# Attention and expert block on one core: spills of batch 2 sent first, w1 ahead of them, a late norm, and eight dummy matmuls

## The chip, the cores and the metric

One NeuronCore of a Trainium2 chip runs the whole program. Five engines work side by side, each through its own instructions in order: TensorE (PE: matmuls, with PEld for the loading of weights), VectorE (DVE), ScalarE (ACT), GpSimd (POOL) and SyncE (SP), which here only starts DMAs. They wait for each other through semaphores. The metric is device time in microseconds, lower is better.

## The reference

Eight batches of 256 tokens by 128 features go through a cross attention block and then a block of 8 experts. The softmax of the attention runs over the head axis, not over the keys.

```python
def _L0_xattn_ref(Q, K, V, W_Q, W_K, W_V, W_O):
    q, k, v = proj_split(Q, W_Q), proj_split(K, W_K), proj_split(V, W_V)   # 8 heads of 16
    scores = jnp.einsum('bhqd,bhkd->bhqk', q, k) / jnp.sqrt(jnp.float32(dh))
    attn = jax.nn.softmax(scores, axis=1)                                   # over the heads
    ctx = jnp.einsum('bhqk,bhkd->bhqd', attn, v)
    return jnp.einsum('bsd,ed->bse', ctx.transpose(0, 2, 1, 3).reshape(b, s, d), W_O)

def _L0_ffn_ref(x, Wr, br, W1, b1, W2, b2):
    logits = jnp.einsum('btd,de->bte', x, Wr) + br
    gates = jax.nn.softmax(jnp.where(top2_mask, logits, neg_inf), axis=-1)
    h = jax.nn.relu(jnp.einsum('btd,edh->bteh', x, W1) + b1)                # all 8 experts
    return jnp.einsum('bte,bteh,ehd->btd', gates, h, W2) + jnp.einsum('bte,ed->btd', gates, b2)

x = x + _L0_xattn_ref(_layernorm(x), ctx_1024, ctx_1024, ...)
x = x + _L0_ffn_ref(_layernorm(x), ...)
```

## The kernel before

Every engine's order is written out by hand. A function `beginning()` per engine lists the first part of the run step by step, and `period(i)` the steady part; `wait_ge` on semaphores joins the engines. A step is called by its batch and part: batches are counted from 0 (so the second batch is number 1), `u` = 0 to 3 is one of the four key and query quarters of a batch, `e` one of the 8 experts.

For one batch the path is this. TensorE projects keys and queries. ScalarE rounds each into a high part and VectorE makes the low part (`k_lo`, `q_lo`: high and low parts keep the precision). SyncE writes them to DRAM ("spill") and reads them back in another layout as `k_stack` and `q_stack`, which `scores(b, u)` multiplies; batch 0 alone has another path without DRAM. VectorE takes the maximum over the heads (`head_max`), TensorE subtracts it (`subtract_max`), ScalarE takes exponentials. The sum over heads is made on TensorE for batch 0 (`head_sum` on PE, with ident) and on GpSimd after that (three additions: `half_sum`, `quarter_sum`, `e_sum`). ScalarE turns the sum into a reciprocal (`invert_sum`: a logarithm, then an exponential), VectorE multiplies (`normalize`, a 128x1024 product of `e_sb` and `e_rcp`). TensorE applies the values and W_O (`attend_values`, `project_out`), VectorE adds the residual and takes statistics (`add_residual`, `ln2`), GpSimd makes the scale and offset (`ln2_end`), ScalarE the normed rows (`make_x1n`), TensorE transposes them (`transpose_x1n`) and starts the experts: `expert_up(b, e)` is six matmuls in `h_ps`, a ReLU on ScalarE follows, then `expert_down(b, e)` into `y_ps`, and `add_expert(b, e)` on VectorE adds the gated result.

The first layer norm works on all 16 row tiles of x (two per batch) in groups. `ln1(lo, hi, at)` on VectorE makes the statistics and the variance of tiles lo to hi; `ln1_rest` on GpSimd waits for that group's variance and makes scale and offset. The last group, `ln1(5 * TT, NT, 4)`, is tiles 10 to 15, that is batches 5 to 7. `split_w1(e)` makes high and low parts of expert e's first weights, on ScalarE and GpSimd.

`expert_down(b, e)` waits until `add_expert` has freed its half of `y_ps`: `wait(pe, gated, j - 1)` with j = 8b + e. In GpSimd's `beginning()` these steps stand in a row: `head_sum(1, 3)`, `ln1_rest(5 * TT, NT, 4)`, `split_w1(5)`, `head_sum(2, 0)`, `split_w1(6)`, `head_sum(2, 1)`, `ln2_end(1)`. In ScalarE's: `relu(0, 4)`, `invert_sum(2, 0)`, `exponentiate(2, 2)`, `relu(0, 5)`, `invert_sum(2, 1)`, `take_k_hi(4)`, `make_x1n(1)`, `relu(0, 6)`. `keep_warm(n)` on TensorE issues n matmuls of the identity whose result nobody reads.

Of the kernel before, what the change touches and what calls it, by code (L numbers as in the profile page):

```python
# [13 lines left out]
P = 128  # L14
# [3 lines left out]
def build(nc, x, ctx_t, w_attn, wr, br, w1, b1_t, w2, b2, out):  # L18
# [3 lines left out]
    TT = S // P  # L22
    NT = B * TT
# [12 lines left out]
    with ExitStack() as stack:  # L36
# [152 lines left out]
        @block.sync  # L189
        def _(sp):  # L190
            def spill_k(b):
                sp.wait_ge(k_hi_made, b)
                sp.wait_ge(k_lo_made, b)
                for part, spilled in enumerate((k_spilled, k_spilled2)):
                    src = k_parts[:, part, :].bitcast(F32).unsqueeze(1).to_broadcast([P, 2, S])
                    sp.dma_start(k_scratch[b % 2, part], src).then_inc(spilled, 16)

            def spill_q(b):
                sp.wait_ge(q_hi_made, b)
                sp.wait_ge(q_lo_made, b)  # L200
                sp.dma_start(q_scratch[b % 2], q_parts[:].bitcast(F32)).then_inc(q_spilled, 16)

            def load_k_stack(b):
                sp.wait_ge(k_spilled, 16 * b)
                sp.wait_ge(k_spilled2, 16 * b)
                if b > 2:
                    sp.wait_ge(scores_done, UNITS * (b - 1))
                for copy in range(2):
                    src = k_scratch[b % 2, copy].rearrange("(j r) c s -> (r c) j s", r=2 * DH)
                    sp.dma_start(k_stack[64 * copy:64 * copy + 64, b % 2, :, :].bitcast(F32),  # L210
                                 src).then_inc(k_stack_in[b % 2], 16)

            def load_q_stack(b):
                sp.wait_ge(q_spilled, 16 * b)
                if b > 2:
                    sp.wait_ge(scores_done, UNITS * (b - 1))
                if b <= 2:
                    sp.wait_ge(q_zeroed[b % 2], 1)
                src = q_scratch[b % 2].rearrange("(j o d) c s -> o (d c) j s", o=2, d=DH)
                for copy in range(2):  # L220
                    for odd in range(2):
                        row = 64 * copy + 32 * odd
                        sp.dma_start(q_stack[row:row + 32, b % 2, :, odd, :].bitcast(F32),
                                     src[odd]).then_inc(q_stack_in[b % 2], 16)

            def store(b):
                sp.wait_ge(gated, E * (b + 1))
                sp.dma_start(out[b].rearrange("(t p) d -> p t d", p=P), y_out[:, b % 2]).then_inc(stored[b % 2], 16)

            def period(i):  # L230
                if there(i - 5):
                    store(i - 5)
                if i - 1 < B:
                    spill_q(i - 1)
                    load_q_stack(i - 1)
                if i < B:
                    spill_k(i)
                    load_k_stack(i)

            x_rows = x.rearrange("b (t p) d -> p (b t) d", p=P)  # L240
            sp.dma_start(x_all[:, 0:TT, :], x_rows[:, 0:TT, :]).then_inc(x0_in, 16)
            sp.dma_start(ctxT[:, 0, :], ctx_t[0]).then_inc(ctx_in[0], 16)
            spill_k(1)
            sp.dma_start(w1_sb[:], w1.rearrange("e d h -> d e h")).then_inc(w1_in, 16)
            load_k_stack(1)
            spill_q(1)
            load_q_stack(1)
            spill_k(2)
            sp.dma_start(ctxT[:, 3:B, :], ctx_t[3:B].rearrange("b d s -> d b s")).then_inc(ctx_rest_in, 16)
            load_k_stack(2)  # L250
            spill_q(2)
            load_q_stack(2)
            sp.dma_start(w2_sb[:], w2.rearrange("e (c p) d -> p (e c) d", p=P)).then_inc(w2_in, 16)
            spill_k(3)
            load_k_stack(3)
            for i in range(4, PERIODS):
                period(i)
            for k in range(2):
                sp.wait_ge(stored[k], 16 * len(range(k, B, 2)))

        @block.tensor
        def _(pe):
            def keep_warm(n):
                for _ in range(n):
                    nc.tensor.matmul(score_ps[:, 1, 0:P], ident[:], ident[:], start=True, stop=True, skip_group_check=True)  # L265

            def project_k(b, freed, n):
                wait(pe, freed, n)
# [69 lines left out]
            def subtract_max(b, u):  # L338
                if UNITS * b + u == 0:
                    pe.wait_ge(neg_ident_made, 1)  # L340
                pe.wait_ge(max_made, UNITS * b + u + 1)
                m4 = shift_m[:, u % 2, :].unsqueeze(1).to_broadcast([P, BANK // P, P])
                for half in range(2):
                    mm = nc.tensor.matmul(score_ps[:, u % 2, half * BANK:(half + 1) * BANK], neg_ident[:], m4,  # L344
                                          start=False, stop=True, skip_group_check=True)
                mm.then_inc(shifted, 1)
# [136 lines left out]
            def beginning():  # L483
# [26 lines left out]
                project_v(1, v_taken, 1)  # L510
                scores(1, 1)
                subtract_max(1, 0)
                attend_values(0, q_lo_made, 2)
                subtract_max(1, 1)
                project_out(0, heads_taken, 1)
                project_v(2, x1_made, 1)
                scores(1, 2)
                scores(1, 3)
                transpose_x1n(0, v_taken, 3)
                subtract_max(1, 2)  # L520
                expert_up(0, 0)
# [312 lines left out]
        def _(dve):  # L834
# [43 lines left out]
            def q_lo(b):  # L878
                low_part(q_parts[:, 1, :], q_bank(b), q_parts[:, 0, :], q_hi_made, b, q_lo_made)
# [161 lines left out]
            def beginning():  # L1041
                dve.wait_ge(x1_in, 16)
                ln1(TT, 2 * TT, 1)
                spread_q(0)
                ln1_end(1, 1)
                k_lo(1)
                spread_q(1)
                head_max(0, 0)
                head_max(0, 1)
                dve.wait_ge(x_in, 16)  # L1050
                ln1(2 * TT, 3 * TT, 2)
                k_lo(2)
                q_lo(1)
                head_max(0, 2)
                ln1(3 * TT, 5 * TT, 3)
                head_max(0, 3)
                normalize(0, 0)
                normalize(0, 1)
                split_wr()
                q_lo(2)  # L1060
                normalize(0, 2)
                head_max(1, 0)
                normalize(0, 3)
                head_max(1, 1)
                ln1(5 * TT, NT, 4)
                add_residual(0)
                ln2(0)
                head_max(1, 2)
                head_max(1, 3)
                x1T_low(0)  # L1070
                normalize(1, 0)
                head_max(2, 0)
                take_logits(0)
                choose_experts(0)
                normalize(1, 1)
                k_lo(3)
                head_max(2, 1)
                make_gates(0)
                transpose_gates(0)
                normalize(1, 2)  # L1080
                normalize(1, 3)
                q_lo(3)
                add_expert(0, 0)
                head_max(2, 2)
                add_expert(0, 1)
                add_expert(0, 2)
                add_b2(0)
                head_max(2, 3)
                add_residual(1)
                ln2(1)  # L1090
                add_expert(0, 3)
                normalize(2, 0)
                k_lo(4)
                head_max(3, 0)
                x1T_low(1)
                add_expert(0, 4)
                add_expert(0, 5)
                take_logits(1)
                normalize(2, 1)
                choose_experts(1)  # L1100
                add_expert(0, 6)
                head_max(3, 1)
                q_lo(4)
                normalize(2, 2)
                add_expert(0, 7)
                normalize(2, 3)
                make_gates(1)
                transpose_gates(1)
                add_expert(1, 0)
                head_max(3, 2)  # L1110
                add_expert(1, 1)
                add_residual(2)
                ln2(2)
                add_expert(1, 2)
                k_lo(5)
                normalize(3, 0)
                add_b2(1)
                head_max(3, 3)
                add_expert(1, 3)
                normalize(3, 1)  # L1120
                x1T_low(2)
                add_expert(1, 4)
# [143 lines left out]
```

## Time and profile before

| what | value |
|---|---|
| median of 3 runs | 211.2 us (210.09 to 212.29) |
| the profiled execution | 212.29 us, span in the profile 210.4 us |
| mean granted clock of TensorE | 0.992 of full speed |
| TensorE busy | 199.6 us, 95% |
| VectorE, ScalarE, GpSimd busy | 80%, 63%, 54% |
| share of the ending chain on TensorE | 91% |

The span is the time between the first and last instruction of the profiled execution; the 1.9 us between it and 212.29 lie around the program. TensorE is busy nearly throughout, and the chain of work that ended last runs through it almost alone from 40 us on. Times in rows are counted from the start of the span.

### The profile page before, as it was taken

Reading aid. Unit: us, or ns where it says so; the run is one execution under the profiler, and the core shown is the slowest. Engines: PE = TensorE matmul, PEld = TensorE weight load, DVE = VectorE, ACT = ScalarE, POOL = GpSimd, SP = SyncE. Lnnn points to the kernel's source line nnn. Section 1 sums busy time; section 2 is a strip of 40 time slices with the busy share of each in tenths; the row PEclk is TensorE's granted clock in tenths of the full one; section 3 lists DMA queues with packets and bytes.
Section 4 is the critical chain, followed back from the end, with each engine's and each line's share of the span. In section 5 each row is a group of like instructions: output and inputs, shape, how many; then the busy total and the mean of one; then the engine's idle time right before and its main releaser. Section 6 shows DMA issues by size and latency. Waiting matters only on the chain.

```text
span 210.4 us, 4952 instructions
## 1 busy us (share of the span) xinstructions
PE 199.6 (95%) x1736; PEld 176.7 (84%) x1736; DVE 167.7 (80%) x453; ACT 132.3 (63%) x316; POOL 112.8 (54%) x132
## 2 busy tenths in 40 slices
PE   6999977698999999999999999999999999999994
PEld 6845865596799978997999889998998899789993
DVE  6388859878798999899888988898999888556532
ACT  2227738678577856877677767587757776345441
POOL 8502838849976397719662856466746674010000
PEclk9999999979999999999999999999999999999999
DMA  6649586805605163315041503332001000000000
GB/s 182 149 121 273 145 258 183 247 4 163 171 19 166 37 174 99 94 34 154 2 153 51 171 7 121 83 126 50 3 0 28 0 2 0 28 3 2 25 3 25
DMA packets 20248, 18.70 MB, mean 89 GB/s; under 512 B 1760, under 2 KB 18688, under 8 KB 20224
## 3 DMA queue, kind: packets, MB, share of 16 engines
q1 hardware_dynamic: 17472, 16.91, 27.9%
q10 hardware_dynamic: 2752, 1.48, 2.8%
q8 instruction: 14, 0.23, 0.5%
q14 instruction: 10, 0.08, 0.1%
HBM read 11.83 MB, written 6.55 MB: 87 GB/s over the span
## 4 chain that ended last, share of the span: by engine, by line
PE 91%; DVE 3%; issue 2%; ACT 2%; POOL 1%; DVEq 0%; POOLq 0%; ACTq 0%
PE y_ps L417 28%; PE h_ps L404 22%; PE score_ps L344 7%; PE misc_ps L363 6%; PE score_ps L332 6%; PE h_ps L352 3%; PE score_ps L265 3%; PE misc_ps L384 2%; PE score_ps L321 2%; PE score_ps L404 2%; PE misc_ps L372 1%; PE misc_ps L270 1%; PE misc_ps L310 1%; PE misc_ps L289 1%; PE misc_ps L283 1%
## 5 line engine op out<-in xcount | busy, mean ns | idle before, releaser
L671 ACT ACTIVATE hT<-h_ps,b_sb 128x256 f32<-128x256 f32 x118 | 49.4, 470 | 34.1 <-PE h_ps L404 33.0
L417 PE MATMUL y_ps<-w_sb,hT 128*128 128x128 f32 x512 | 68.5, 277 | 0.0
L417 PEld LDWEIGHTS y_ps<-w_sb,hT 128*128 128x128 f32 x512 | 63.3, 191 | 3.4 <-issue 2.2
L1156 POOL TENSOR_TENSOR half_sum<-e_sb 128x512 f32<-128x512 f32 x28 | 37.2, 1328 | 32.0 <-ACT e_sb L643 31.7
L912 DVE TENSOR_TENSOR attn<-e_sb,e_rcp 128x1024 f32<-128x1024 f32 x32 | 42.2, 1321 | 3.3 <-ACT e_rcp L654 3.3
L904 DVE TENSOR_REDUCE shift_m<-score_ps 128x128 fp32r<-128x1024 f32 x32 | 38.7, 1213 | 4.0 <-PE score_ps L332 2.8
L404 PE MATMUL h_ps<-x1T_hi,w_lo 128*128 128x256 f32 x118 | 38.1, 323 | 1.3 <-ACT hT L671 0.6
L643 ACT ACTIVATE e_sb<-score_ps 128x1024 f32<-128x1024 f32 x32 | 32.8, 1024 | 5.6 <-PE score_ps L344 5.4
L978 DVE SCALAR_TENSOR_TENSOR acc<-y_ps,gates,acc 128x128 f32<-128x128 f32 x96 | 29.1, 343 | 8.6 <-PE y_ps L417 7.3
L404 PE MATMUL h_ps<-x1T_hi,w_hi 128*128 128x256 f32 x118 | 33.3, 283 | 0.0
L404 PE MATMUL h_ps<-x1T_lo,w_hi 128*128 128x256 f32 x118 | 33.3, 282 | 0.0
L1158 POOL TENSOR_TENSOR quarter_sum<-half_sum 128x256 f32<-128x256 f32 x28 | 27.5, 983 | 2.2
L404 PEld LDWEIGHTS h_ps<-x1T_hi,w_lo 128*128 128x128 f32 x118 | 22.6, 192 | 4.2 <-issue 2.0
L404 PEld LDWEIGHTS h_ps<-x1T_lo,w_hi 128*128 128x128 f32 x118 | 22.6, 192 | 0.3
L404 PEld LDWEIGHTS h_ps<-x1T_hi,w_hi 128*128 128x128 f32 x118 | 22.6, 191 | 0.0
L332 PE MATMUL score_ps<-q_stack,k_stack 128*128 128x256 f32 x112 | 20.0, 303 | 1.9 <-issue 1.9
L344 PE MATMUL score_ps<-shift_m,neg_ident 128*128 128x512 f32 x64 | 21.8, 421 | 0.0
L1161 POOL TENSOR_TENSOR e_sum<-quarter_sum 128x128 f32<-128x128 f32 x28 | 17.6, 629 | 2.2
L332 PEld LDWEIGHTS score_ps<-q_stack,k_stack 128*128 128x128 f32 x112 | 15.4, 194 | 2.4 <-issue 2.3
L1167 POOL TENSOR_TENSOR ln_rstd<-ln_var,neg_half 128x2 f32<-128x2 f32 x8 | 5.7, 707 | 21.0 <-DVE ln_var L871 21.0
L363 PE MATMUL misc_ps<-attn,v_pad 128*32 128x256 f32 x256 | 15.5, 382 | 0.6 <-issue 0.6
L344 PEld LDWEIGHTS score_ps<-shift_m,neg_ident 128*128 128x128 f32 x64 | 10.1, 193 | 3.1 <-issue 2.8
(112 smaller groups left out, 286.3 us busy)
## 6 DMA issues: line engine op xcount, KB each, us to landing
k_scratch<-k_parts SPq DMA_DIRECT2D x14, 256.0 KB, 2.6
k_stack<-k_scratch SPq DMA_DIRECT2D x14, 256.0 KB, 3.9
q_stack<-q_scratch SPq DMA_DIRECT2D x28, 128.0 KB, 2.7
q_scratch<-q_parts SPq DMA_DIRECT2D x7, 256.0 KB, 2.1
w_sb<-in_w SPq DMA_DIRECT2D x1, 1024.0 KB, 7.1
out_y<-y_out SPq DMA_DIRECT2D x8, 128.0 KB, 1.9
x_all<-in_x ACTq DMA_DIRECT2D x1, 768.0 KB, 6.1
ctxT<-in_ctx_t SPq DMA_DIRECT2D x1, 640.0 KB, 5.1
```

The costliest lines, as they stand in the source:

```text
L332: mm = nc.tensor.matmul(score_ps[:, u % 2, 2 * j * P:(2 * j + 2) * P], k_stack[:, b % 2, j, kt * P:(kt + 1) * P], q_stack[:, b % 2, j, :, ...
L344: mm = nc.tensor.matmul(score_ps[:, u % 2, half * BANK:(half + 1) * BANK], neg_ident[:], m4, start=False, stop=True, skip_group_check=True)
L363: mm = nc.tensor.matmul(misc_ps[32 * g:32 * g + 32, 0:S], v_pad[:, b % 4, kt, h, :], attn[:, b % 2, kt, h, :], start=(odd == 0 and kt == 0 ...
L404: mm = nc.tensor.matmul(hidden(j)[:, c * S:(c + 1) * S], w[:, e, c * P:(c + 1) * P], xt[:, b % 2, :], start=(k == 0), stop=(k == 2))
L417: mm = nc.tensor.matmul(y_ps[:, j % 2, t * D:(t + 1) * D], hT[:, j % 2, c, t * P:(t + 1) * P], w2_sb[:, e * HC + c, :], start=(c == 0), st ...
L643: nc.scalar.activation(e_sb[:, u, :], score_ps[:, u % 2, :], ACT.Exp, scale=SCALE).then_inc(exp_made, 1)
L671: op = nc.scalar.activation(hT[:, j % 2, c, :], hidden(j)[:, c * S:(c + 1) * S], ACT.Relu, bias=b1_sb[:, e * HC + c:e * HC + c + 1])
L904: nc.vector.tensor_reduce(shift_m[:, u % 2, :], score_ps[:, u % 2, :].rearrange("p (h q) -> p q h", h=H), AX.X, ALU.max).then_inc(max_made, 1)
L912: nc.vector.tensor_tensor(attn[:, b % 2, kt, :, qt * P:(qt + 1) * P], e_sb[:, u, :].rearrange("p (h q) -> p h q", h=H), e_rcp[:, u, :].uns ...
L978: op = nc.vector.scalar_tensor_tensor(out=dst, in0=y_ps[:, j % 2, t * D:(t + 1) * D], scalar=gates[:, b % 2, t, e:e + 1], in1=src[:, t, :] ...
L1156: nc.gpsimd.tensor_tensor(half_sum[:], e[:, 0:HQ // 2], e[:, HQ // 2:HQ], ALU.add).then_inc(sum_step, 1)
L1158: nc.gpsimd.tensor_tensor(quarter_sum[:], half_sum[:, 0:HQ // 4], half_sum[:, HQ // 4:HQ // 2], ALU.add).then_inc(sum_step, 1)
```

## The change

Three edits. On SyncE the load of w1 goes ahead of the first spill and gets two waits of its own (`x1_in` and `ctx_in[1]`, two input loads that ScalarE starts), and the spill of the queries of batch 1 goes ahead of its key stack load. On VectorE the statistics of tiles 10 to 15 move from before `add_residual(0)` to behind `q_lo(3)`. On TensorE a new function `fill` issues 2, 2 and 4 dummy matmuls in three places; its wait is for `q_lo_made` of batch 1.

```diff
             sp.dma_start(ctxT[:, 0, :], ctx_t[0]).then_inc(ctx_in[0], 16)
+            sp.wait_ge(x1_in, 16)
+            sp.wait_ge(ctx_in[1], 16)
+            sp.dma_start(w1_sb[:], w1.rearrange("e d h -> d e h")).then_inc(w1_in, 16)
             spill_k(1)
-            sp.dma_start(w1_sb[:], w1.rearrange("e d h -> d e h")).then_inc(w1_in, 16)
+            spill_q(1)
             load_k_stack(1)
-            spill_q(1)
             load_q_stack(1)
...
+            def fill(times):
+                pe.wait_ge(q_lo_made, 1)
+                for _ in range(times):
+                    nc.tensor.matmul(y_ps[:, 0, 0:P], ident[:], ident[:], start=True, stop=True, skip_group_check=True)
...
                 subtract_max(1, 0)
+                fill(2)
                 attend_values(0, q_lo_made, 2)
                 subtract_max(1, 1)
                 project_out(0, heads_taken, 1)
+                fill(2)
                 project_v(2, x1_made, 1)
                 scores(1, 2)
                 scores(1, 3)
+                fill(4)
                 transpose_x1n(0, v_taken, 3)
...
                 head_max(1, 1)
-                ln1(5 * TT, NT, 4)
                 add_residual(0)
...
                 q_lo(3)
+                ln1(5 * TT, NT, 4)
                 add_expert(0, 0)
```

SyncE's queue at its start, before: `k_scratch` and `q_scratch` are the spills of batch 1, `w_sb` is w1, `k_stack` and `q_stack` the loads that `scores(1, 0)` waits for.

```order
3 L196 DMA k_scratch<-k_parts 256x1x256 [waits k_lo_made,k_hi_made]
4 L196 DMA k_scratch<-k_parts 256x1x256
5 L244 DMA w_sb<-in_w 128x8x256
6 L210 DMA k_stack<-k_scratch 64x4x256 [waits k_spilled2,k_spilled]
7 L210 DMA k_stack<-k_scratch 64x4x256
8 L201 DMA q_scratch<-q_parts 128x512 [waits q_lo_made,q_hi_made]
9 L223 DMA q_stack<-q_scratch 32x4x256 [waits q_zeroed1,q_spilled]
```

The same place of the changed kernel:

```order
3 L245 DMA w_sb<-in_w 128x8x256 [waits ctx1_in,x1_in]
4 L196 DMA k_scratch<-k_parts 256x1x256 [waits k_lo_made,k_hi_made]
5 L196 DMA k_scratch<-k_parts 256x1x256
6 L201 DMA q_scratch<-q_parts 128x512 [waits q_lo_made,q_hi_made]
7 L210 DMA k_stack<-k_scratch 64x4x256 [waits k_spilled2,k_spilled]
8 L210 DMA k_stack<-k_scratch 64x4x256
9 L223 DMA q_stack<-q_scratch 32x4x256 [waits q_zeroed1,q_spilled]
```

w1 now stands first, and the query spill stands before the two key stack loads.

VectorE around `add_residual(0)` (L857) before; L912 is `normalize(0, 3)`, L904 `head_max(1, 1)`, and L837 to L844 the statistics of tiles 10 to 15:

```order
40 L912 TENSOR_TENSOR attn<-e_sb,e_rcp 128x8x128 [waits rcp_made]
41 L904 TENSOR_REDUCE shift_m<-score_ps 128x128 [waits scores_done]
42 L837 BN_STATS ln_stats<-x_all 128x6 x6
43 L841 BN_AGGR ln_mv<-ln_stats 128x2 [waits ln1_step]
44 L841 BN_AGGR ln_mv<-ln_stats 128x2 x5
45 L844 TENSOR_SCALAR ln_var<-ln_mv 128x6 [waits ln1_step]
46 L857 TENSOR_TENSOR x<-misc_ps,x_all 128x256 [waits wo_done]
```

VectorE between the products of batch 1 and the first expert's result, in the changed kernel (L922 is `normalize(1, 2)` and `(1, 3)`, L886 `q_lo(3)`, L988 `add_expert(0, 0)`):

```order
69 L922 TENSOR_TENSOR attn<-e_sb,e_rcp 128x8x128 [waits rcp_made] x2
70 L886 TENSOR_TENSOR q_parts<-misc_ps,q_parts 128x256 [waits q_hi_made]
71 L847 BN_STATS ln_stats<-x_all 128x6 x6
72 L851 BN_AGGR ln_mv<-ln_stats 128x2 [waits ln1_step]
73 L851 BN_AGGR ln_mv<-ln_stats 128x2 x5
74 L854 TENSOR_SCALAR ln_var<-ln_mv 128x6 [waits ln1_step]
75 L988 SCALAR_TENSOR_TENSOR acc<-y_ps,gates,x 128x128 [waits gates_made,y_done]
```

The four rows of the statistics now follow `q_lo(3)` and precede the first use of an expert's result; nothing stands between `head_max(1, 1)` and `add_residual(0)` any more.

GpSimd from `head_sum(1, 3)` to `ln2_end(1)` in the changed kernel (L1149 to L1158 is `ln1_rest(5 * TT, NT, 4)`, L1184 `split_w1(5)` and `(6)`, L1177 `ln2_end(1)`):

```order
38 L1171 TENSOR_TENSOR e_sum<-quarter_sum 128x128 [waits sum_step]
39 L1149 TENSOR_TENSOR ln_rstd<-ln_var,neg_half 128x6 [waits ln1_var_made]
40 L1154 TENSOR_TENSOR ln_neg<-ln_mv,minus_one 128x6
41 L1158 TENSOR_TENSOR ln_off<-ln_neg,ln_rstd 128x6 [waits ln1_rstd_made,ln1_off_step]
42 L1184 TENSOR_TENSOR w_lo<-w_sb,w_hi 128x256 [waits w1_hi_made]
43 L1166 TENSOR_TENSOR half_sum<-e_sb 128x512 [waits exp_made]
44 L1168 TENSOR_TENSOR quarter_sum<-half_sum 128x256 [waits sum_step]
45 L1171 TENSOR_TENSOR e_sum<-quarter_sum 128x128 [waits sum_step]
46 L1184 TENSOR_TENSOR w_lo<-w_sb,w_hi 128x256 [waits w1_hi_made]
47 L1166 TENSOR_TENSOR half_sum<-e_sb 128x512 [waits exp_made]
```

Nothing moved here: the order is that of before, with `ln1_rest` in the same place in the row.

## Rows read from the trace of the kernel before

**Rows 1.** The page: the granted clock of TensorE in 40 slices, in tenths.

```profile
PEclk9999999979999999999999999999999999999999
```

**Rows 2.** Timeline of TensorE: start us, us, line, tile; in brackets idle before.

```profile
7.90 1.28 PE L265 MATMUL score_ps<-ident 128*128 128x128 f32 x10
...
27.80 0.72 PE L332 MATMUL score_ps<-q_stack,k_stack 128*128 128x256 f32 x4 [1.90 <-issue]
...
32.31 1.93 PE L363 MATMUL misc_ps<-attn,v_pad 128*32 128x256 f32 x32 [0.61 <-issue]
...
34.83 0.68 PE L372 MATMUL misc_ps<-w_qkvo,headsT 128*128 128x128 f32 x4
36.03 0.71 PE L310 MATMUL misc_ps<-w_qkvo,ctxT 128*128 128x128 f32 x4 [0.52 <-DVE x L857]
...
39.10 0.41 PE L283 MATMUL misc_ps<-ident,x1n 128*128 128x128 f32 x2 [1.41 <-ACT x1n L597]
```

**Rows 3.** By window: PE, PEld, DVE, ACT, POOL busy; then granted clock, DMA share, GB/s.

```profile
41.00:42.00 1.00, 1.00 (x8) 1.00 (x7) 0.70 (x1) 0.55 (x3) 0.87 (x1) 0.64 0.80 219
42.00:43.00 1.00, 1.00 (x7) 1.00 (x7) 0.66 (x1) 0.97 (x4) 0.92 (x2) 0.50 0.01 4
...
44.00:45.00 1.00, 1.00 (x6) 0.86 (x5) 0.93 (x9) 0.53 (x2) 0.19 (x1) 0.65 0.00 0
```

**Rows 4.** Timeline of SyncE's DMA issues; then its waits (total us, times, longest).

```profile
15.89 1.29 SPq L210 DMA_DIRECT2D k_stack<-k_scratch  x2
17.43 0.40 SPq L201 DMA_DIRECT2D q_scratch<-q_parts  x1
23.44 1.76 SPq L223 DMA_DIRECT2D q_stack<-q_scratch  x4
...
SPq L223 <- DMA q_scratch<-q_parts: 16.9, 7, 5.5
...
q_stack<-q_scratch SPq DMA_DIRECT2D x28, 128.0 KB, 2.7
```

**Rows 5.** Timeline of VectorE around both places of the moved statistics.

```profile
33.26 1.25 DVE L837 BATCH_NORM_STATS2 ln_stats<-x_all 128x6 f32<-128x128 f32 x6
...
35.55 0.42 DVE L857 TENSOR_TENSOR x<-misc_ps,x_all 128x256 f32<-128x256 f32 x1
...
52.57 0.42 DVE L876 TENSOR_TENSOR q_parts<-misc_ps,q_parts 128x256 fp32r<-128x256 f32 x1
52.91 0.60 DVE L978 SCALAR_TENSOR_TENSOR acc<-y_ps,gates,x 128x128 f32<-128x128 f32 x2
```

**Rows 6.** Timeline of GpSimd: late scale and offset, splits, sums, and `ln2_end(0)`.

```profile
37.07 0.71 POOL L1167 TENSOR_TENSOR ln_rstd<-ln_var,neg_half 128x2 f32<-128x2 f32 x1 [0.98 <-DVE ln_var L871]
...
49.59 1.33 POOL L1139 TENSOR_TENSOR ln_rstd<-ln_var,neg_half 128x6 f32<-128x6 f32 x1
...
52.63 0.73 POOL L1174 TENSOR_TENSOR w_lo<-w_sb,w_hi 128x256 fp32r<-128x256 f32 x1
...
55.49 0.46 POOL L1161 TENSOR_TENSOR e_sum<-quarter_sum 128x128 f32<-128x128 f32 x1
...
57.95 0.72 POOL L1158 TENSOR_TENSOR quarter_sum<-half_sum 128x256 f32<-128x256 f32 x1
58.75 0.45 POOL L1161 TENSOR_TENSOR e_sum<-quarter_sum 128x128 f32<-128x128 f32 x1
...
99.42 1.60 POOL L1158 TENSOR_TENSOR quarter_sum<-half_sum 128x256 f32<-128x256 f32 x1
```

**Rows 7.** Timeline of ScalarE: `make_x1n(0)`, then the step of `invert_sum(2, 0)`.

```profile
38.08 0.88 ACT L597 ACTIVATE x1n<-x,ln_off,ln_rstd 128x128 f32<-128x128 f32 x2 [0.92 <-POOL ln_off L1170]
...
57.13 0.31 ACT L652 ACTIVATE log_sum<-e_sum 128x128 f32<-128x128 f32 x1
```

**Rows 8.** Timeline of TensorE: `attend_values(1)`, then the last work ahead of `transpose_x1n(1)`.

```profile
53.28 1.93 PE L363 MATMUL misc_ps<-attn,v_pad 128*32 128x256 f32 x32
...
62.40 1.05 PE L417 MATMUL y_ps<-w_sb,hT 128*128 128x128 f32 x8
```

## The prediction

> **What bounds the kernel now.** I read four views in this order: the page for busy shares and clock, the chain of waits, the timelines of all engines from 20 to 70 us, and the queue of SyncE. TensorE is busy 95% of the span and carries 91% of the ending chain, so a change pays only where it lets TensorE's row of work start earlier and stay early to the end. From 45 us to the end TensorE hardly stops, so a gain won before 45 us is kept unless a new wait eats it. The gaps worth having lie between 25.9 and 39.1 us: 1.90 us ahead of `scores(1, 0)`, then 0.61, 0.52 and 1.41 us [rows 2]. Behind them the page shows its only low digit in the granted clock [rows 1]; by window it is 0.50, TensorE's lower level of 1.2 GHz, from 42 us, and 0.64 in the microsecond before, so it fell near 41.3 us; 0.65 in the microsecond from 44 says that it was back at 2.4 GHz at about 44.7 us [rows 3]. That is 3.4 us at half rate. In the 15 us before the fall TensorE had stood idle for 4.9 us in all (those four, and 0.46 us ahead of `expert_up(0, 0)`).
>
> **The DMA edit.** `scores(1, 0)` starts at 27.80 us, though TensorE was free 1.90 us before that, at 25.90 [rows 2]. It waits for the query stack: that load was issued at 23.44 us, because the query spill, issued at 17.43 behind w1 and the key stack loads, had taken 5.5 us to land; over all seven batches this wait sums to 16.9 us [rows 4]. The first two batches took 5.5 and 3.4 us of it, the other five 1.6 us each. In the changed order the spill is again issued at 17.4 us (it waits for `q_lo(1)`), now with w1 gone. With 1.6 to 3.4 us to land, the stack load's four issues (1.76 us) begin at 19.4 to 21.2 and end at 21.2 to 23.0, and with 2.7 us to landing the data is there at 23.9 to 25.7 us. Both are ahead of 25.9, so the whole 1.9 us goes. The price is small: the key stack loads are issued near 17.9 instead of 15.89 us, still 2 us before the query stack's. w1 itself goes out near 6 us, beside the last part of x, and is read on ScalarE from about 20.7 us. Loads that share the early engines with it have slack: the rest of x is used first at 15.5 us.
>
> **The dummies.** Ten records, which are five calls of `keep_warm`, took 1.28 us at full clock [rows 2], so two calls cost at most 0.51 us and four 1.02 us. They stand in gaps of 0.61, 0.52 and 1.41 us that end by waits of other engines (VectorE's product, `add_residual(0)`, ScalarE's `make_x1n(0)`), which the dummies don't touch. They cost nothing; with an overlap of a few hundredths the bound is 0.1 us. If those gaps shrank they would cost up to 2.0 us, but the first edit moves both ends of each gap alike: everything from `head_sum(0, 3)` to `make_x1n(0)` hangs on `scores(1, 0)`, and moves 1.9 us as one piece.
>
> **The clock.** With the 1.9 us gap gone and 1.8 us of the other 2.5 filled, TensorE is idle for under 1 us in those 15 us instead of 4.9. I take it that the clock stays at 2.4 GHz. The ends of that term are 0 and 1.7 us (half of 3.4). I take 1.35: `expert_up(0, 1)` can't start before the ReLU of `expert_up(0, 0)`, and the exponential of quarter 3 of batch 1 stands behind two ReLUs and a layer norm on ScalarE, which holds `scores(2, 1)` to about 1.35 us earlier. So work up to `q_lo(3)` gains 1.9 + 1.35 = 3.25 us.
>
> **The moved statistics: what they free.** They lie from 33.26 to 35.55 us on VectorE, right before `add_residual(0)` [rows 5]. But `add_residual` also needs `project_out(0)`, which ends at 34.83 + 0.68 = 35.51 [rows 2]. What is late next comes 0.04 us behind. Taking 2.3 us away there brings nothing.
>
> **What they cost.** Two things wait for them in the new place. The first is `add_expert(0, 0)`. Before, it began as `q_lo(3)` ended (52.99 us) and was done at 53.51 [rows 5]; `expert_down(0, 2)` needs it, and TensorE came there at 55.21, behind `attend_values(1)` [rows 8], with 1.7 us in hand. The 2.3 us use this up and leave a stall of 0.6 us. The second is GpSimd. Its `ln1_rest` of the same tiles began at 49.59 us with the variance 14 us old [rows 6]. Now it must wait for it, and two weight splits, the sums of quarters 0 and 1 of batch 2 and `ln2_end(1)` are queued behind it; ScalarE's `invert_sum(2, 0)`, which waits for the first of these sums, has the next exponential, ReLU and `make_x1n(1)` behind it. So I add the path from the end of `q_lo(3)` to `transpose_x1n(1)`:
>
> - statistics 2.3 us [rows 5]
> - `ln1_rest` 1.3 us. Before, it took 52.63 - 49.59 = 3.04 us with two of VectorE's `normalize` beside it; `ln2_end(0)`, one power and one product, took 1.0 us from its start to the start of the engine that waited for it [rows 6, 7], and a second small product makes about 1.1. In the new place VectorE reads PSUM in `add_expert` and `head_max`, so I stay near 1.1
> - split, sum, split, sum: 59.20 - 52.63 = 6.6 us [rows 6]
> - one collision: `normalize(2, 0)`, behind `add_residual(1)` and `ln2(1)` on VectorE, now falls at about 58 us, onto `head_sum(2, 1)`. A `quarter_sum` beside a `normalize` took 1.60 us instead of 0.72 [rows 6]: 0.9 us, with 0 as its other end
> - `ln2_end(1)` to the start of the normed rows 38.08 - 37.07 = 1.0 us, and from there to the transposes 39.10 - 38.08 = 1.0 us [rows 2, 6, 7]
>
> Together 13.1 us. `q_lo(3)` would end at 52.99 - 3.25 = 49.74, and the transposes start at 62.85 us. Before, TensorE reached them at 62.40 + 1.05 = 63.45 us [rows 8]. Only 0.6 us is left of 3.25. Said as one rule: gain = (lead at `q_lo(3)`) - 2.7 us. The stall at `expert_down(0, 2)` is absorbed in this longer one of about 2 us. Behind 63.45 us everything goes on as before, 0.6 us earlier. Without the collision it is 1.5, with `ln1_rest` at its dear end -1.1.
>
> The collision is the place where a rule of the notes bears. The row shows 0.9 us more for a GpSimd addition that met one VectorE product. The Trainium skill ("SBUF — State Buffer", section "SBUF: two separate sides") says that the two engines share one port pair as an exclusive lock, which a VectorE operation with two SBUF inputs holds for its whole length while GpSimd stops. By that rule the price would be nearly a full product, 1.2 us, and the gain 0.3 us; by the row it is 0.6.
>
> **The sum.** 212.29 us of the profiled execution less 0.6 is 211.7. That execution lay 1.1 us over the median of 211.2, which is my base: 210.6 us.
>
> **The rivals.**
>
> A, GpSimd doesn't hold the transposes. ScalarE reached `invert_sum(2, 0)` at 57.13 us, while GpSimd's sum had ended at 55.95 [rows 6, 7]; such a slack of 1.2 us speaks for it, and my 13.1 us has seven terms. Then only the stall of 0.6 us counts: 3.25 - 0.6 = 2.65 us, 208.6 us. Chance 0.20.
>
> B, the clock still falls, there or near the new stalls at 52 and 61 us, since the rows show one fall alone and not what the chip asks for. For it speaks that a fall can have other causes than these gaps, of which no row tells; against it that idle time shrinks by four fifths. Lead 1.9, so 0.8 us slower: 212.0 us. Chance 0.13.
>
> C, slower. The mechanism is GpSimd's wait for the late variance, and it costs 2.7 us whatever is won ahead. It decides as soon as the lead at `q_lo(3)` is below 0.6 us: if the query stack still lands late, because spill and key loads share the engines, and the clock falls too. At a lead of 0 it is 211.2 + 2.7 = 213.9 us. Chance 0.10.
>
> That the dummies fill nothing, since their gaps are gone, is part of A: they would add at most 2.0 us.
>
> **How the numbers follow.** My forecast has 0.57, A 0.20, B 0.13, C 0.10. One per cent, 2.1 us, is about what a measurement of this kernel can tell from no change. Forecast and B lie within it, A is faster, C slower: 0.20, 0.70, 0.10. The range runs from a little under A's time, 208.3, to a little over B's, 212.5, which leaves out C and the ends of A where the collision is missing and the stall too.
>
> **What the new profile would show.** Right: `scores(1, 0)` starts at 25.9 us with no wait; no digit under 9 in the clock; `q_lo(3)` ends near 49.7; VectorE's six statistics follow; GpSimd idles from about 46.5 to 52.1 us ahead of `ln_rstd`; ScalarE waits for `e_sum` at `invert_sum(2, 0)` and `(2, 1)`; TensorE waits 0.6 us at `expert_down(0, 2)` and about 2 us before `transpose_x1n(1)`, which starts at 62.9. Wrong: no GpSimd release in front of ScalarE near 56 to 61 us (A), or a stretch at 0.50 (B). The prediction fails most easily in the 13.1 us: 1 us less there is 1 us more gain.

## The result, and the profile after

The changed kernel is 0.7% slower: 211.86 us median (210.71 to 212.68, 21 runs) against 210.20 us (209.28 to 213.21, 21 runs) of the kernel before beside it, ratio 1.0073, 95% interval 1.0056 to 1.0089, so +1.2 to +1.9 us. The profiled execution took 211.71 us, span 209.8. Forecast were 210.6 us and a small gain.

The page of the changed kernel, busy shares and granted clock [rows 1]:

```profile
PE 200.3 (95%) x1752; PEld 176.7 (84%) x1752; DVE 168.7 (80%) x453; ACT 131.8 (63%) x316; POOL 111.1 (53%) x132
...
PEclk9999999999999999999999999999999999999999
...
PE 86%; POOL 5%; DVE 4%; ACT 2%; issue 1%; DVEq 0%; POOLq 0%; ACTq 0%
```

The last line is the ending chain's share by engine: GpSimd stands in it with 5%. The timeline of SyncE's DMA issues [rows 4]:

```profile
17.16 0.34 SPq L201 DMA_DIRECT2D q_scratch<-q_parts  x1
17.59 1.29 SPq L210 DMA_DIRECT2D k_stack<-k_scratch  x2
19.20 1.76 SPq L223 DMA_DIRECT2D q_stack<-q_scratch  x4
```

The query stack load goes out at 19.20 instead of 23.44 us. TensorE's timeline [rows 2, 8]:

```profile
25.49 0.71 PE L339 MATMUL score_ps<-q_stack,k_stack 128*128 128x256 f32 x4
...
30.04 1.93 PE L370 MATMUL misc_ps<-attn,v_pad 128*32 128x256 f32 x32 [0.15 <-issue]
...
36.84 0.41 PE L290 MATMUL misc_ps<-ident,x1n 128*128 128x128 f32 x2 [0.52 <-ACT x1n L607]
...
52.18 1.13 PE L424 MATMUL y_ps<-w_sb,hT 128*128 128x128 f32 x8 [0.37 <-DVE acc L988]
...
62.76 0.41 PE L290 MATMUL misc_ps<-ident,x1n 128*128 128x128 f32 x2 [1.82 <-ACT x1n L607]
```

The wait ahead of `scores(1, 0)` is gone, the dummies have filled the gaps, and two new waits stand behind 50 us: `expert_down(0, 2)` and, of 1.82 us, `transpose_x1n(1)`. Behind the latter the timeline shows no further wait of TensorE. VectorE [rows 5]:

```profile
49.17 0.42 DVE L886 TENSOR_TENSOR q_parts<-misc_ps,q_parts 128x256 fp32r<-128x256 f32 x1
49.51 1.25 DVE L847 BATCH_NORM_STATS2 ln_stats<-x_all 128x6 f32<-128x128 f32 x6
...
57.23 0.17 DVE L881 TENSOR_SCALAR ln_var<-ln_mv 128x2 f32<-128x2 f32 x1
57.30 1.28 DVE L882 TENSOR_SCALAR ln_neg<-ln_mv 128x2 f32<-128x2 f32 x1
58.50 0.60 DVE L988 SCALAR_TENSOR_TENSOR acc<-y_ps,gates,acc 128x128 f32<-128x128 f32 x2
59.02 1.44 DVE L922 TENSOR_TENSOR attn<-e_sb,e_rcp 128x1024 f32<-128x1024 f32 x1
```

GpSimd, then ScalarE, on the path from `q_lo(3)` to the transposes [rows 6, 7]:

```profile
51.59 1.33 POOL L1149 TENSOR_TENSOR ln_rstd<-ln_var,neg_half 128x6 f32<-128x6 f32 x1 [5.38 <-DVE ln_var L854]
...
53.33 0.72 POOL L1184 TENSOR_TENSOR w_lo<-w_sb,w_hi 128x256 fp32r<-128x256 f32 x1
...
57.29 1.27 POOL L1166 TENSOR_TENSOR half_sum<-e_sb 128x512 f32<-128x512 f32 x1
58.64 0.74 POOL L1168 TENSOR_TENSOR quarter_sum<-half_sum 128x256 f32<-128x256 f32 x1
59.45 1.32 POOL L1171 TENSOR_TENSOR e_sum<-quarter_sum 128x128 f32<-128x128 f32 x1
60.73 0.70 POOL L1177 TENSOR_TENSOR ln_rstd<-ln_var,neg_half 128x2 f32<-128x2 f32 x1
```

```profile
56.67 0.31 ACT L662 ACTIVATE log_sum<-e_sum 128x128 f32<-128x128 f32 x1 [2.42 <-POOL e_sum L1171]
...
60.80 0.31 ACT L662 ACTIVATE log_sum<-e_sum 128x128 f32<-128x128 f32 x1 [1.84 <-POOL e_sum L1171]
...
61.74 0.88 ACT L607 ACTIVATE x1n<-x,ln_off,ln_rstd 128x128 f32<-128x128 f32 x2
```

GpSimd idles 5.38 us for the late variance, and ScalarE then waits twice for a sum: 2.42 and 1.84 us.

The two profiled executions, 212.29 before and 211.71 after, differ by just the 0.6 us of gain that the prediction gave. The medians go the other way, so the study asks which execution of before is the usual one, what each edit is worth alone, and whether it is GpSimd or VectorE that costs. For every kernel the same two distances are read: end of `q_lo(3)` to the start of `transpose_x1n(1)` (D), and from there to the end of the span (147.0 to 147.2 us in 11 of the 14 profiles read, before and after among them; 147.7 in e6, which was not followed up, 147.9 in e9 and 148.4 in e11, told below).

### The profile page after: what moved, and what is told of

The parts are those of the page before. It is cut to its first block, busy times and chain, and to the rows that moved or that the text cites. A ratio compares the mean times of both kernels' runs of the same rounds, so it can differ in the third digit from the quotient of the medians.

```text
span 209.8 us, 4985 instructions
## 1 busy us (share of the span) xinstructions
PE 200.3 (95%) x1752; PEld 176.7 (84%) x1752; DVE 168.7 (80%) x453; ACT 131.8 (63%) x316; POOL 111.1 (53%) x132
## 4 chain that ended last, share of the span: by engine, by line
PE 86%; POOL 5%; DVE 4%; ACT 2%; issue 1%; DVEq 0%; POOLq 0%; ACTq 0%
PE y_ps L424 26%; PE h_ps L411 20%; PE score_ps L351 7%; PE misc_ps L370 6%; PE score_ps L339 5%; PE h_ps L359 4%; PE score_ps L267 3%; PE score_ps L328 2%; PE misc_ps L391 2%; PE score_ps L411 2%; PE misc_ps L379 2%; PE misc_ps L277 1%; POOL half_sum L1166 1%; DVE attn L922 1%; PE misc_ps L317 1%
## 5 line engine op out<-in xcount | busy, mean ns | idle before, releaser
L922 DVE TENSOR_TENSOR attn<-e_sb,e_rcp 128x1024 f32<-128x1024 f32 x32 | 42.4, 1327 | 2.1 <-ACT e_rcp L664 2.1
L988 DVE SCALAR_TENSOR_TENSOR acc<-y_ps,gates,acc 128x128 f32<-128x128 f32 x96 | 29.1, 344 | 7.6 <-PE y_ps L424 6.1
L1171 POOL TENSOR_TENSOR e_sum<-quarter_sum 128x128 f32<-128x128 f32 x28 | 18.5, 659 | 2.2
L1177 POOL TENSOR_TENSOR ln_rstd<-ln_var,neg_half 128x2 f32<-128x2 f32 x8 | 5.7, 707 | 20.0 <-DVE ln_var L881 20.0
```

Of the source, the lines that this page charges most:

```text
L922: nc.vector.tensor_tensor(attn[:, b % 2, kt, :, qt * P:(qt + 1) * P], e_sb[:, u, :].rearrange("p (h q) -> p h q", h=H), e_rcp[:, u, :].uns ...
L988: op = nc.vector.scalar_tensor_tensor(out=dst, in0=y_ps[:, j % 2, t * D:(t + 1) * D], scalar=gates[:, b % 2, t, e:e + 1], in1=src[:, t, :] ...
```

## The experiments

The kernel before ran beside each. e1 to e4 shared one chip, e5 to e8 a second, e9 to e12 a third.

**e1, the kernel before once more.** No edit.

> The kernel before, unchanged. Theory (clock): the prediction took its profiled execution of 212.29 us as typical, but that one had the clock fall near 41 us and the median run of before does not; this profile and most of its runs then show a granted clock of 1.0, a time near 210.2 us, and the lead of the changed kernel at the end of q_lo(3) is 1.3 to 1.9 us instead of 3.25. Rival (the change itself costs something that isn't seen at 63 us): the profile shows a clock of 0.99 again and 211 to 212 us.

Measured: 210.58 us against 210.61, ratio 0.9992 (0.9965 to 1.0020). The profiled execution (210.63 us) is the one that explains the case. The end of its first wait, `q_lo(3)` and the transposes, then a window at the place of the fall (us, PE busy, clock, DMA share, GB/s):

```profile
27.35 0.71 PE L332 MATMUL score_ps<-q_stack,k_stack 128*128 128x256 f32 x4 [1.23 <-issue]
...
50.97 0.42 DVE L876 TENSOR_TENSOR q_parts<-misc_ps,q_parts 128x256 fp32r<-128x256 f32 x1
...
61.69 0.38 PE L283 MATMUL misc_ps<-ident,x1n 128*128 128x128 f32 x2
```

```profile
42.00:43.00 1.00, 0.94 (x7) 1.00 0.00 0
```

In the second block the clock is 1.00 where [rows 3] have 0.50. The wait is 1.23 instead of 1.90 us. From the start of `scores(1, 0)` to the end of `q_lo(3)` it took 24.04 us, against 25.19 in the execution that the prediction was made on. The fall cost 1.15 us between these two executions. How often it comes, the mean clocks tell. In the 65 runs of before beside the experiments, on three chips, it was 0.999 or 1.000 in 37 (medians 210.26, 210.41 and 209.99 us by chip), 0.992 in 22 (211.11, 211.10, 210.81) and lower in 6. In e1's own 12 runs it was 0.992 or lower in 7, which is against the expectation that most would stand at 1.0. So 35 of 77 runs of this kernel had a fall: on the chip of e1 17 of 29, on the other two 14 of 31 and 4 of 17. The fall is in somewhat under half of the runs, and a median pays only a part of it.

**e2, the statistics late, nothing else.**

```diff
                 head_max(1, 1)
-                ln1(5 * TT, NT, 4)
                 add_residual(0)
...
                 q_lo(3)
+                ln1(5 * TT, NT, 4)
```

> Before with the statistics of tiles 10 to 15 behind q_lo(3), nothing else. Theory (GpSimd waits for the late variance, gain = lead - 2.7 us): the lead is 0, so it is 2.2 to 2.9 us slower than before, ScalarE waits over 2 us for e_sum at each of invert_sum(2, 0) and (2, 1), and TensorE stands still ahead of transpose_x1n(1). Rival (the DMA order or the dummies cost the time): within 0.5 us of before.

Measured: 214.34 us, ratio 1.0189 (1.0160 to 1.0218); +3.7 us, more than expected. From VectorE and TensorE:

```profile
50.61 0.42 DVE L876 TENSOR_TENSOR q_parts<-misc_ps,q_parts 128x256 fp32r<-128x256 f32 x1
...
64.20 0.41 PE L283 MATMUL misc_ps<-ident,x1n 128*128 128x128 f32 x2 [1.81 <-ACT x1n L597]
```

D is 64.20 - 51.03 = 13.17 us, exactly that of the changed kernel, against 10.30 in e1 (61.69 - 51.39): +2.87. The other 0.8 us are not explained by the clock: five of six runs had 0.991 or 0.992, but the one at 1.000 was the slowest (214.99 us), and the profiled one, whose clock fell near 39 us, the fastest (213.03). e11 runs the same kernel again.

**e3, the order of spills and loads alone.** The first hunk of the diff of the change, nothing else.

> Before with w1 and the query spill moved on SyncE, nothing else. Theory: the wait of 1.9 us ahead of scores(1, 0) is gone and nothing takes it back: 1.5 to 1.9 us faster than before. Rival (w1 or the later key loads cost something further on): under 0.7 us faster, or slower.

Measured: 208.87 us, ratio 0.9923 (0.9901 to 0.9945), the clock 1.000 in all six runs. `scores(1, 0)` starts without a wait, and D is 10.29.

**e4, that edit and the dummies; e5, the dummies alone.** The first and third, then only the third part of the change.

> The changed kernel with the statistics back in their old place. Theory: as the run with the DMA edit alone, 1.5 to 1.9 us faster than before, and the clock falls in fewer executions. Rival (the dummies are in the way): slower than the DMA edit alone by 0.5 us or more. If both this and the DMA edit alone are near 1.7 us faster, the moved statistics alone cost the changed kernel about 3.2 us.

> Before with the eight dummy matmuls alone. Theory (the dummies lie in gaps and the clock rarely falls in the median run): within 0.4 us of before, all gaps from 0.5 to 1.4 us smaller by the dummies' time. Rival (they hold the clock up, which is worth 1.4 us): 1 us or more faster. Rival (they delay the work behind them): 0.5 us or more slower.

Measured: e4 209.15 us, 0.9935 (0.9911 to 0.9958), e5 209.59 against 210.97, 0.9957 (0.9932 to 0.9983). The gain of e5, 0.9 us by the ratio, is more than the 0.4 us of the expectation. In e5 the clock was 0.997 or more in all 12 runs, where 14 of the 31 runs of before beside it stood at 0.992 or lower. So with the dummies alone the fall is away; behind the DMA edit, whose runs all stand at 1.000 without them, they add nothing that can be told (0.9935 and 0.9923, intervals overlap).

**e6, the changed kernel with GpSimd's `ln1_rest` behind `ln2_end(1)`.** The queue behind the late variance is taken away.

```diff
                 head_sum(1, 3)
-                ln1_rest(5 * TT, NT, 4)
                 split_w1(5)
...
                 ln2_end(1)
+                ln1_rest(5 * TT, NT, 4)
```

> The changed kernel with GpSimd's ln1_rest of tiles 10 to 15 moved behind ln2_end(1), so that nothing urgent is queued behind its wait; VectorE's order stays as changed. Theory (GpSimd's wait is the cost): the distance from the end of q_lo(3) to transpose_x1n(1) falls from 13.17 us to 10.8 to 11.2, that is 2.0 to 2.4 us faster than the changed kernel, 0.3 to 0.8 us faster than before; only the stall of 0.4 us at expert_down(0, 2) stays. Rival (VectorE's own delay of 1.9 us is the cost): the same as the changed kernel within 0.5 us.

Measured: 212.32 us, 1.0069 (1.0042 to 1.0096). The forecast gain didn't come, but D did fall, from 13.17 to 63.58 - 52.11 = 11.47 us, a clock fall (below) included (10.8 to 11.2 were expected), so GpSimd's wait had been what held the transposes. What came instead lies ahead of `q_lo(3)`: GpSimd now ran its split and sums early, into VectorE's row of small operations and its two products. VectorE, TensorE, then GpSimd in e6:

```profile
46.62 0.69 DVE L963 TENSOR_TENSOR gated_onehot<-onehot,gate_of 128x32 f32<-128x32 f32 x1
47.35 1.18 DVE L966 TENSOR_TENSOR gates<-gated_onehot 128x16 f32<-128x16 f32 x1
...
48.73 3.05 DVE L922 TENSOR_TENSOR attn<-e_sb,e_rcp 128x1024 f32<-128x1024 f32 x2
...
52.17 3.34 PE L370 MATMUL misc_ps<-attn,v_pad 128*32 128x256 f32 x32 [1.88 <-DVE q_parts L886]
...
46.53 0.73 POOL L1184 TENSOR_TENSOR w_lo<-w_sb,w_hi 128x256 fp32r<-128x256 f32 x1
47.22 1.27 POOL L1166 TENSOR_TENSOR half_sum<-e_sb 128x512 f32<-128x512 f32 x1
...
49.38 1.31 POOL L1171 TENSOR_TENSOR e_sum<-quarter_sum 128x128 f32<-128x128 f32 x1
50.65 1.71 POOL L1184 TENSOR_TENSOR w_lo<-w_sb,w_hi 128x256 fp32r<-128x256 f32 x1
```

The same place of e1:

```profile
48.07 0.19 DVE L953 TENSOR_TENSOR gated_onehot<-onehot,gate_of 128x32 f32<-128x32 f32 x1
48.30 0.17 DVE L956 TENSOR_TENSOR gates<-gated_onehot 128x16 f32<-128x16 f32 x1
...
48.68 2.32 DVE L912 TENSOR_TENSOR attn<-e_sb,e_rcp 128x1024 f32<-128x1024 f32 x2
...
47.98 1.33 POOL L1139 TENSOR_TENSOR ln_rstd<-ln_var,neg_half 128x6 f32<-128x6 f32 x1
```

`gates` takes 1.18 instead of 0.17 us, and ends with `half_sum` (48.53 and 48.49). `gated_onehot` takes 0.50 us more, and the two products 0.73 us more. Together that is 2.24 of the 2.3 us by which the stretch from `scores(1, 0)` to `q_lo(3)` grew (26.38 us, 24.10 in the changed kernel). In e1 it is the long `ln_rstd` that runs there, and the small operations keep their short times. TensorE stood still for 1.88 us for this, and its clock fell near 51.7 us, inside that stall, so `attend_values(1)` took 3.34 instead of 1.93 us; 3 of the 8 runs stood at 0.992.

**e7, the DMA edit with `ln1_rest` ahead of `head_sum(1, 3)`.** Statistics early, as in e3.

```diff
+                ln1_rest(5 * TT, NT, 4)
                 head_sum(1, 3)
-                ln1_rest(5 * TT, NT, 4)
```

> Before with the DMA edit, and GpSimd's ln1_rest of tiles 10 to 15 one step earlier, ahead of head_sum(1, 3), where GpSimd was idle for 1.6 us. Theory (from 45 us on TensorE's own work sets the end): the same as the DMA edit alone within 0.4 us. Rival (GpSimd's lateness costs something even in the old order): 0.5 us or more faster than the DMA edit alone.

Measured: 210.90 against 210.97 us, 1.0000 (0.9974 to 1.0025), so some 1.6 us worse than e3 by the ratios. The same collision: `gates` 1.18 us, and `q_lo(3)` ends 26.69 us behind the start of `scores(1, 0)` instead of 24.01. Here too the clock fell behind the stall it makes (2.19 us, until 51.26), near 52.6 us, and D was 11.61 for e3's 10.29. Five of 12 runs stood at 0.991 (211.53 to 211.96 us), the others at 1.000 (210.59 to 210.94), so the loss is in part the collision and in part the clock.

**e8, the changed kernel without its dummies.** The three calls of `fill` are taken out.

> The changed kernel without its dummies (DMA edit and late statistics). Theory (the dummies are worth nothing in the median): within 0.4 us of the changed kernel, so 1.1 to 1.9 us slower than before. Rival (the dummies keep the clock up): more executions under a granted clock of 1.0 and 0.7 us or more slower than the changed kernel.

Measured: 212.04 us, 1.0048 (1.0024 to 1.0072), D 13.18. The interval overlaps that of the changed kernel: in it the dummies are worth nothing that can be told.

**e9, VectorE's delay alone; e10, GpSimd's wait alone.** Both on e4, whose used statistics are early. e9 computes six statistics, their aggregates and the variance a second time, into spare tiles that nobody reads; e10 adds one wait, until `add_expert(0, 1)` is done.

```diff
                 q_lo(3)
+                spare_ln1()
                 add_expert(0, 0)
```

```diff
                 head_sum(1, 3)
+                pool.wait_ge(gated, 2)
                 ln1_rest(5 * TT, NT, 4)
```

> The kernel with the DMA edit and the dummies (209.15 us, 0.9935 of before), and behind q_lo(3) on VectorE a second set of six-tile statistics into spare tiles that nobody reads; the statistics that are used stay in their early place. This is VectorE's share of the late statistics (1.8 us behind q_lo(3)) without GpSimd's wait. My theory (what costs is GpSimd's chain behind ln_var, and VectorE's delay makes only a stall of 0.4 to 0.6 us at expert_down): 209.4 to 209.9 us, ratio 0.994 to 0.999, and from the end of q_lo(3) to transpose_x1n(1) between 10.4 and 11.1 us. Rival (it is VectorE's delay that costs, and GpSimd's wait only happens beside it): 211.3 to 212.0, distance near 13.

> The kernel with the DMA edit and the dummies, and one added wait: GpSimd holds ahead of ln1_rest(5*TT,...) until the second add_expert of the first batch has run on VectorE, some 1.9 us behind q_lo(3), which is where ln_var releases it in the changed kernel. The statistics stay early. This is GpSimd's wait without VectorE's delay. My theory: nearly all of the cost is here, 211.3 to 212.1 us, ratio 1.003 to 1.009, the distance from the end of q_lo(3) to transpose_x1n(1) 12.6 to 13.2 us, and an e_sum of 1.3 us beside normalize. Rival (VectorE's delay costs): 209.1 to 209.6, distance near 10.5.

Measured: e9 210.71 us, 1.0027 (1.0004 to 1.0050), where 0.994 to 0.999 was expected; e10 212.24 us, 1.0110 (1.0081 to 1.0138); before 210.02. TensorE in e9:

```profile
52.85 1.13 PE L428 MATMUL y_ps<-w_sb,hT 128*128 128x128 f32 x8 [0.88 <-DVE acc L1003]
...
61.19 0.38 PE L294 MATMUL misc_ps<-ident,x1n 128*128 128x128 f32 x2
```

And in e10, TensorE, GpSimd and VectorE:

```profile
63.30 0.41 PE L290 MATMUL misc_ps<-ident,x1n 128*128 128x128 f32 x2 [1.80 <-ACT x1n L607]
...
52.12 1.33 POOL L1149 TENSOR_TENSOR ln_rstd<-ln_var,neg_half 128x6 f32<-128x6 f32 x1 [5.62 <-DVE acc L988]
...
59.18 1.59 POOL L1168 TENSOR_TENSOR quarter_sum<-half_sum 128x256 f32<-128x256 f32 x1
...
57.90 2.28 DVE L922 TENSOR_TENSOR attn<-e_sb,e_rcp 128x1024 f32<-128x1024 f32 x1
```

GpSimd's wait alone makes D 63.30 - 49.88 = 13.42 us, the whole cost (+3.1) and 0.25 more than late statistics (12.6 to 13.2 were expected), because `ln_rstd` starts 2.24 us behind `q_lo(3)` here, and 2.00 in the changed kernel. It was `quarter_sum` that met `normalize`, and not `e_sum`. VectorE's delay alone makes it 61.19 - 49.76 = 11.43 (+1.1), more than the 0.4 to 0.6 that I gave it: its last small operation, the variance, took 0.69 instead of 0.17 us and ended at 52.18 with a `quarter_sum` of GpSimd (52.17). The two costs don't add (13.17 in the changed kernel, where the sum would be 14.5), so they are two paths to the same transposes, and the longer one, GpSimd's, is what the change pays. e9's time is higher than its D says: against e12 2.3 us, of which the profiles explain 1.1 by D, 0.4 by a later `q_lo(3)`, and 0.8 by the last store, for whose landing SyncE waited 2.2 us in e9 and 1.4 in every other profile. Whether that store is late in e9's usual run is open.

**e11, e2 again; e12, e3 again.**

> The kernel of e2 again (before with the statistics alone behind q_lo(3)), which came out 3.7 to 4.0 us slower where the cost term says 2.7. If the term is right and the rest was the state of that chip's runs: 1.3 ppt of ratio, 1.011 to 1.015, 212.9 to 213.6 us. If the late statistics cost more without the DMA edit (as the shorter lead of the second batch would have it): 1.017 to 1.021 again, and the profile shows where beyond the 13.2 us from q_lo(3) to transpose_x1n(1).

> The kernel of e3 again (the order of spills and loads alone), for the size of its gain and as the best version: 208.5 to 209.3 us, ratio 0.990 to 0.995. If e3 was the luck of a chip, 0.995 to 1.0.

Measured: e11 213.03 us, 1.0138 (1.0104 to 1.0172), so +2.9 us, near the 2.87 of D and within the expectation. Of its six runs the two at clock 1.0 took 212.2 and 212.5 us, the four at 0.991 and 0.992 213.0 to 214.3. The profiled one (214.26 us) has D = 13.21 and 148.4 us behind the transposes instead of 147.1. By window, columns as in e1:

```profile
63.00:64.00 1.00, 0.00 (x0) 1.00 0.00 0
64.00:65.00 1.00, 0.99 (x6) 1.00 0.19 65
65.00:66.00 1.00, 1.00 (x8) 0.59 1.04 344
66.00:67.00 1.00, 1.00 (x5) 0.50 0.35 116
67.00:68.00 1.00, 1.00 (x7) 0.50 0.00 0
68.00:69.00 1.00, 1.00 (x6) 0.70 0.57 163
```

The clock fell near 65.2 us, 1.2 us behind the end of the 1.83 us stall that the late statistics make, and this execution is 1.3 us longer behind the transposes. So the edit can have a second cost, a second place where the clock falls. It is seen in this one profile; e2's profile has its fall at the old place, and why e2 came out 0.8 us dearer than e11 stays open. e12: 208.42 us, 0.9920 (0.9892 to 0.9947), the clock 1.000 in all six runs. The DMA edit alone is the best kernel of the study, 1.6 us under before on two chips.

## Why the prediction was wrong

**The failed step is the base and the lead that was set against it**: "So work up to `q_lo(3)` gains 1.9 + 1.35 = 3.25 us", and then "That execution lay 1.1 us over the median of 211.2, which is my base". Both terms were read from an execution that the usual run isn't like. Its wait was 1.90 us, where the other profiles with the old DMA order have 1.23, 1.09, 1.13 and 0.89 (e1, e2, e5, e11). Its clock fell, for 1.15 us, where 42 of 77 runs of before show next to no fall. I had credited the end of the fall in full to the median, which pays only a part of it. The sum that should have stood there: 1.1 to 1.2 us of wait and, from e3 and e12, some 0.4 us of clock on the mean, 1.6 us of lead; less 2.9. That is 1.3 us slower, and 1.2 to 1.9 were measured. Two estimates fit this: 35 of 77 runs with a fall, at 0.7 to 0.85 us between the medians, make 0.3 to 0.4 us on the mean, and the changed kernel's own falls, below, take some 0.2 us back.

e1's profile and that of the changed kernel differ in the same way: `q_lo(3)` ends 1.80 us earlier (51.39 and 49.59), D costs 2.87, and 1.80 - 2.87 = -1.07; the times are 210.63 and 211.71. But of the 1.80 us only 1.23 are the wait. Another 0.63 is that TensorE was free for `scores(1, 0)` at 25.49 instead of 26.12 us, which differs from execution to execution and not with the order of the DMAs: 24.76 to 26.12 us in the five profiles with the old order, 24.52 to 26.09 in the nine with the new.

That 211.86 us lies near the forecast of 210.6, and near B's 212.0, is in part luck. The base of three runs, 211.2 us, was 1.0 us over the median of the 21 beside the change; less 0.6 from 210.20 would have been 209.6.

**The DMA edit** was right: the load at 19.20 us lies at the early end of the 19.2 to 21.2 I gave, and no wait is left in e3, e12 or the changed kernel, 0.23 us in e4.

**The dummies** cost nothing that can be told, as forecast. Behind the DMA edit they weren't needed: e3 and e12 hold the clock without them. Alone, in e5, they were worth 0.9 us.

**The clock** term was right as a mechanism and over-sized, 1.15 for 1.35, and wrong as a full gain of the median. Falls also came in 7 of the changed kernel's 21 runs (clocks 0.990 to 0.997, median 212.29 against 211.72 us). Where the clock fell in those no profile shows; e11's did behind the stall.

**What the statistics free**: nothing, as forecast. From the start of `scores(1, 0)` to the end of `q_lo(3)` it took 24.02 us in e11, and 24.04 in e1.

**What they cost**: the path was right step by step, the total 13.17 for 13.1. Read from the rows above: statistics to `ln_rstd` 51.59 - 49.59 = 2.00 (2.3), `ln1_rest` 53.33 - 51.59 = 1.74 (1.3, my most doubtful term), four steps and the collision 60.73 - 53.33 = 7.40 (7.5), the last two 2.03 (2.0). But D of before is 10.30, not 10.46, since the transposes' own row says 63.29 us and I had taken the modelled end of the matmul ahead [rows 8]. The edit costs 2.87 for 2.7. The stall at `expert_down(0, 2)` was 0.37 for 0.6.

**The collision.** The row gave 0.9 us, and 1.32 - 0.46 = 0.86 us came. The Trainium skill ("SBUF — State Buffer", section "SBUF: two separate sides") says that whichever of the two engines starts first holds the port pair for its whole instruction. For sums and products the trace agrees, and it shows why my use of the rule, a full product of 1.2 us, was too dear: `normalize` was itself held first (1.44 for 1.22 us), ended at 60.46, and `e_sum`, which had started at 59.45, ended 0.31 us behind that. For GpSimd's `ln_rstd` the trace does not agree: `gated_onehot`, which has two inputs in SBUF, took its 0.19 us beside it in e1, where the rule would have it wait.

**The rivals.** A fell: GpSimd holds ScalarE twice. B's time, 212.0 us, was met for another reason, since the clock was at 1.00 throughout the changed kernel's profile and in 14 of its 21 runs; its lead of 1.9, without a clock term, came nearer to the 1.6 of the runs than my 3.25. C's mechanism is the one that decided: the wait costs its 2.9 us whatever is won ahead. C's condition, a lead under 0.6 us, did not come; a lead under 2.9 was enough for the kernel to be slower.

## What to carry to other kernels

Before a wait or a clock fall of one profiled execution is booked as a gain, ask what part of it the median pays: the mean clocks of the other runs and a second profile of the same kernel told it here. A producer moved "to where it is free" is paid by everything queued in order behind its consumer; for that, find the next point where the bound engine meets that queue, and compare the two distances to it. Apply edits that win and edits that don't one at a time: here the DMA order alone won 1.6 us, and the late statistics took 2.9.

## What the runs showed of the hardware

GpSimd's sums hold up even VectorE's smallest operations with SBUF operands: `ln_neg` (128x2) 1.28 for 0.16 us and `gates` (128x16) 1.18 for 0.17, each ending with a `half_sum`, while `ln_rstd` (128x6, 1.33 us) let two of them through at 0.19 and 0.17. So VectorE's small operations kept their short times here while GpSimd was idle (the changed kernel) or in `ln_rstd` (e1), and sums pulled into that gap delayed TensorE's path, by 2.3 us in e6. Why `ln_rstd` lets them through, no run tells. In one and the same kernel TensorE's clock falls in some runs and not in others: near 41 us in the first profile of before, and not in e1. In the profiles of e6, e7 and e11 it fell beside one long stall: inside the 1.88 us of e6, 1.3 us behind the 2.19 us of e7 and 1.2 us behind the 1.83 us of e11, in the last two while TensorE was fully busy again. The changed kernel's profile has such a stall too, of 1.82 us, and no fall.
